# Scattering part of the edges, moving record groups between stages, and turning edge attributes in pairs in a graph network kernel

## The reference, cut to what matters

```python
edge_index = jnp.stack([src, dst])
x = x + _L0_gnn_ref(_layernorm(x), edge_index, ...)   # two gin convolutions
x = x + _L0_ffn_ref(...)                              # slice attention
x = x + _L1_gnn_ref(...)                              # graph attention
x = x + _L1_ffn_ref(...)                              # 8 experts, 2 per node
x = x + _L2_gnn_ref(..., edge_attr_64, ...)           # edge update, below
x = x + _L2_ffn_ref(...)                              # 32 experts, 1 per node
x = x + _L3_gnn_ref(..., src, dst, edge_type_8)       # relations
x = x + _L3_ffn_ref(...)

def _gin_conv(x, src, dst, n, W1, b1, gamma, beta, W2, b2):
    agg = jax.ops.segment_sum(x[src], dst, num_segments=n)
    h = jax.nn.relu(_batchnorm((x + agg) @ W1 + b1, gamma, beta))
    return jax.nn.relu(h @ W2 + b2)

# in _L2_gnn_ref, with row, col = edge_index
edge_in = jnp.concatenate([h[row], h[col], edge_attr], axis=-1)
msg = jax.nn.relu(edge_in @ W1.T + b1) @ W2.T + b2
agg = jax.ops.segment_sum(msg, row, num_segments=h.shape[0])
```

## Time and profile before

| | |
|---|---|
| median of 3 runs | 5867.91 us (5867.34 to 5868.26) |
| the profiled execution | 5852.53 us |
| its span, from the first to the last instruction | 5850.8 us |
| busy: PE, DVE, ACT, POOL | 4793.1, 3170.6, 1333.6, 3178.7 us |
| mean granted clock of TensorE | 0.879 of 2.4 GHz |
| stage of placing | about 93 to 331 us of the span |
| edge update, the loop over quads | about 3672 to 4330 us of the span |

### The profile page before, as it was taken

One profiled execution on the slowest core, in us unless ns is written; L12 is line 12 of the kernel. 1 busy time (PEld: TensorE's weight loads), 2 busy tenths in 40 slices (PEclk: granted clock), 3 DMA queues, 4 the chain that ended last, 5 costly groups with the idle time before them and its releaser, 6 DMA issues. The chain is left out here.

```text
span 5850.8 us, 74399 instructions
## 1 busy us (share of the span) xinstructions
PE 4793.1 (82%) x20458; PEld 2904.0 (50%) x20459; DVE 3170.6 (54%) x7606; ACT 1333.6 (23%) x3259; POOL 3178.7 (54%) x3560
## 2 busy tenths in 40 slices
PE   7968887788768599979985998999997678888674
PEld 2223434433345411118864997788874433333364
DVE  8964444444355577768984114566667433444432
ACT  4940002000032222222213333333332121000121
POOL 3237774777615577746633776667630212777324
PEclk7979999999978755559997999999998789999887
DMA  5013332333411267765525765333330533333265
GB/s 214 11 56 105 103 104 66 106 105 105 95 29 37 78 204 216 216 198 149 159 79 187 219 219 153 112 115 114 114 73 1 154 118 125 105 105 104 50 195 170
DMA packets 392381, 711.85 MB, mean 122 GB/s; under 512 B 117999, under 2 KB 257327, under 8 KB 391663
## 3 DMA queue, kind: packets, MB, share of 16 engines
q0 software_dynamic: 131680, 340.14, 21.3%
q1 hardware_dynamic: 257152, 364.49, 19.5%
q10 hardware_dynamic: 3216, 3.28, 0.2%
HBM read 532.97 MB, written 174.69 MB: 121 GB/s over the span
## 5 line engine op out<-in xcount | busy, mean ns | idle before, releaser
L795 PE MATMUL ps<-wide 128*128 128x256 f32 x2640 | 915.2, 429 | 309.8 <-DMA wide<-table,src 179.8
L822 DVE TENSOR_TENSOR wide<-wide,ps 128x256 f32 x1320 | 555.0, 420 | 968.2 <-PE ps L795 965.2
L780 POOL DMA_INDIRECT wide<-table,src x880 | 846.0, 961 | 276.5 <-PE ps L795 205.0
L795 PEld LDWEIGHTS ps<-wide 128*128 128x128 f32 x2640 | 405.4, 189 | 834.4 <-DMA wide<-table,src 547.4
L792 PE MATMUL ps<-zerow,zerob 128*128 128x440 bf16 x2640 | 712.1, 352 | 27.8 <-DVE wide L127 27.8
L780 POOL DMA_INDIRECT wide<-table_rel,rel x440 | 423.4, 962 | 332.4 <-ACTq L96 198.7
L2777 POOL DMA_INDIRECT work<-table,work x440 | 448.3, 1019 | 190.9 <-issue 106.7
L1669 POOL DMA_INDIRECT wide<-table_gat,src x440 | 427.0, 970 | 135.3 <-issue 133.9
L792 PEld LDWEIGHTS ps<-zerow,zerob 128*128 128x128 bf16 x2640 | 259.2, 98 | 221.9 <-DVE wide L127 29.5
L1838 POOL TENSOR_TENSOR wide<-wide,work 128x1024 f32<-128x1024 f32 x110 | 222.2, 2020 | 197.3 <-ACT work L1822 197.3
L1763 DVE TENSOR_REDUCE work<-ps 128x8 f32<-128x1024 f32 x220 | 269.0, 1223 | 103.9 <-PE ps L1729 100.2
(11 more groups left out here) (522 smaller groups left out, 8647.0 us busy)
## 6 DMA issues: line engine op xcount, KB each, us to landing
edge_rows<-wide SPq DMA_DIRECT2D x110, 532.0 KB, 3.2
wide<-edge_rows SPq DMA_DIRECT2D x110, 532.0 KB
normed<-in_L_ffn_W SPq DMA_DIRECT2D x42, 1024.0 KB
table_rel<-wide SPq DMA_DIRECT2D x25, 1024.0 KB, 4.4
wide<-in_L_ffn_expert_w SPq DMA_DIRECT2D x90, 256.0 KB, 3.1
work<-rec SPq DMA_DIRECT2D x110, 136.0 KB, 2.1
rec<-work SPq DMA_DIRECT2D x27, 544.0 KB, 16.3
normed_T<-in_L_ffn_W SPq DMA_DIRECT2D x14, 1024.0 KB
```

The source lines that it names most:

```text
L780: nc.gpsimd.indirect_dma_start(rows[:, w % RT, :], None, table, bass.IndirectOffsetOnAxis(ap=index[:, w:w + 1], axis=0)).then_inc(gathered ...
L795: nc.tensor.matmul(m.PS[:, w % (2 * Q), 0:D], S[:, w % RT, :], rows[:, w % RT, :], start=True, stop=True).then_inc(summed, 1)
L822: v.tensor_tensor(at, at, m.PS[:, s, 0:D], ALU.add).then_inc(added, 1)
```

## The change

Three things are changed.

First, in `place_edges`, the first 112 of the 416 edge tiles (`STRAIGHT`) no longer go through one-hot products. POOL scatters their two numbers (8 bytes a row) to a table in DRAM, `placed`, that was filled with zeros in an earlier stage; SP loads the table back (`back`), and DVE adds it to what the products of the other 304 tiles gave. For that DVE makes the index `where`, and `pairs`, ahead of its loop, and has two more additions behind it. POOL does its scatters ahead of the record groups.

Second, only groups 0 to 2 are sent in `place_edges`. Groups 3 and 4 go to `linear_features` of the first convolution, 5 and 6 to that of the second, 7 and 8 to `gin_output` of the second. Their loads stand on SP behind the stage's own weights. Groups from 9 stay where they were.

Third, in `edge_update`, SP loads attributes and ends with two DMAs into two buffers, so that the attributes of two edge tiles lie side by side: 128 columns. PE turns such a pair with one transpose instead of two. `wa` becomes 128x512 with the 64x256 weights twice on its diagonal, and one product of 512 columns serves two edge tiles. POOL fills it with zeros, and SP waits for that before it loads the weights and then the records.

```diff
-PLACED = 9
+PLACED = 3
+IN_GIN = 2
+STRAIGHT = 112
+BEGUN = PLACED + 3 * IN_GIN
@@ place_edges
-            for t in range(ET):
+            for t in range(STRAIGHT, ET):
...
         def _(pool):
+            pool.wait_ge(m.placed_blanked, 16)
+            pool.wait_ge(paired, 3)
+            for t in range(STRAIGHT):
+                nc.gpsimd.indirect_dma_start(m.placed, bass.IndirectOffsetOnAxis(ap=where_i[:, t:t + 1], axis=0),
+                                             pairs[:, t, :], None).then_inc(scattered, 16)
             pool.wait_ge(m.rec_blanked, 16 * -(-WP // (BLANK // 4)))
...
+            sp.wait_ge(scattered, 16 * STRAIGHT)
+            sp.dma_start(back, m.placed.rearrange("(p w) c -> p w c", p=P)).then_inc(returned, 16)
...
+            c.step(v.scalar_tensor_tensor(where, m.row_e[:, first], float(WP), m.col_e[:, first], ALU.mult, ALU.add))
+            v.tensor_copy(where_i, where).then_inc(paired, 1)
+            v.tensor_copy(pairs[:, :, 0], both[:, first]).then_inc(paired, 1)
+            v.tensor_copy(pairs[:, :, 1], near[:, first]).then_inc(paired, 1)
...
-            c2.step(v.tensor_tensor(code, below[0][:, 1:WP], below[0][:, 0:WT], ALU.subtract))
-            c2.step(v.scalar_tensor_tensor(source, below[1][:, 1:WP], float(HALF), below[1][:, 0:WT], ALU.add,
-                                           ALU.subtract))
+            dve.wait_ge(returned, 16)
+            c2.step(v.tensor_tensor(upper[0], below[0][:, 1:WP], back[:, 0:WT, 0], ALU.add))
+            c2.step(v.scalar_tensor_tensor(upper[1], below[1][:, 1:WP], float(HALF), back[:, 0:WT, 1], ALU.add, ALU.add))
+            c2.step(v.tensor_tensor(code, upper[0], below[0][:, 0:WT], ALU.subtract))
+            c2.step(v.tensor_tensor(source, upper[1], below[1][:, 0:WT], ALU.subtract))
@@ the groups in the convolutions
+class RecordsBeside:
...
+    def loads(self, sp):
+        for u, g in enumerate(self.groups):
+            load_group(sp, self.attr, self.records, g, u, self.arrived)
+
+    def sends(self, pool):
+        send_groups(self.nc, pool, self.m, self.records, self.groups, self.arrived, self.sent, self.filled)
+        for u in range(IN_GIN):
+            pool.wait_ge(self.sent[u], 16 * SG)
@@ edge_update
-            sp.dma_start(wa[0:EA, :], w1[2 * D:2 * D + EA, :]).then_inc(loaded, 16)
+            sp.wait_ge(blanked, 1)
+            for side in range(2):
+                sp.dma_start(wa[side * EA:(side + 1) * EA, side * D:(side + 1) * D], w1[2 * D:2 * D + EA, :]
+                             ).then_inc(loaded, 16)
...
-                sp.dma_start(rec[:, u * Q:(u + 1) * Q, :], r[:, bass.ds(j * Q, Q), :]).then_inc(came[u], 16)
+                sp.dma_start(ends[:, u * Q:(u + 1) * Q, :], r[:, bass.ds(j * Q, Q), EA:EA + 2]).then_inc(came[u], 16)
+                sp.dma_start(attrs[:, u * Q * EA:(u + 1) * Q * EA].rearrange("p (s c) -> p s c", s=Q),
+                             r[:, bass.ds(j * Q, Q), 0:EA]).then_inc(came[u], 16)
...
-                    mm = te.transpose(m.PS[0:EA, 1, s * P:(s + 1) * P], rec[:, u * Q + s, 0:EA], m.ident[:])
+                for k in range(PAIRS):
+                    at = (u * PAIRS + k) * P
+                    mm = te.transpose(m.PS[:, 1, k * P:(k + 1) * P], attrs[:, at:at + P], m.ident[:])
...
-                    te.matmul(at, ST[:, k, :], tile_at(by_src, tiles[s]), start=True, stop=False)
-                    mm = te.matmul(at, attT[:, k, :], wa, start=False, stop=True)
+                for k in range(PAIRS):
+                    te.matmul(m.PS[:, 2 + k, :], attT[:, u % RS * PAIRS + k, :], wa, start=True, stop=False)
+                    for s in range(2 * k, 2 * k + 2):
+                        at = m.PS[:, 2 + k, s % 2 * D:(s % 2 + 1) * D]
+                        mm = te.matmul(at, ST[:, u % RS * Q + s, :], tile_at(by_src, tiles[s]), start=False,
+                                       stop=(s % 2 == 1))
```

More of the change, by code:

```diff
@@ L458, in place_edges @@
         below = [view(m.BB, o + 5 * WT + ET + k * WP, WP) for k in range(2)]
+        o += 5 * WT + ET + 2 * WP
+        upper = [view(m.BB, o + k * WT, WT) for k in range(2)]
+        back = view(m.BB, o + 2 * WT, WP, 2)
+        pairs = view(m.BB, o + 2 * WT + 2 * WP, STRAIGHT, 2)
+        where = view(m.BB, o + 2 * WT + 2 * WP + 2 * STRAIGHT, STRAIGHT)
+        where_i = view(m.BB, o + 2 * WT + 2 * WP + 3 * STRAIGHT, STRAIGHT).bitcast(I32)
+        first = slice(0, STRAIGHT)
         block = st.block()
@@ L521, in _ @@
                           skip_group_check=True)
-            for t in range(ET):
-                pe.wait_ge(hot, t + 1)
-                pe.wait_ge(stepped, t + 1)
+            for t in range(STRAIGHT, ET):
+                pe.wait_ge(hot, t - STRAIGHT + 1)
+                pe.wait_ge(stepped, t - STRAIGHT + 1)
                 for k in range(2):
@@ L562, in send_groups, with __init__, prepare @@
             after(n)
+class RecordsBeside:
+    def __init__(self, nc, m, attr, first, at):
+        self.nc, self.m, self.attr = nc, m, attr
+        self.groups = range(first, first + IN_GIN)
+        self.records = view(m.WS, at, IN_GIN * SG, EA + 4)
+    def prepare(self, st):
+        self.arrived, self.sent, self.filled = st.sems("arrived", IN_GIN), st.sems("sent", IN_GIN), st.sem("filled")
+    def loads(self, sp):
[5 more added lines that the diff above has]
+            pool.wait_ge(self.sent[u], 16 * SG)
 def blank_records(nc, pool, m, buf, blanked, stored):
@@ L966, in _, with linear_features @@
                 nc.vector.tensor_copy(dst[:, t, :], m.PS[:, t % U, 0:D]).then_inc(taken, 1)
-def linear_features(nc, m, srcT, weight, bias, dstT, gamma, beta):
+def linear_features(nc, m, srcT, weight, bias, dstT, gamma, beta, beside):
     BANKS = 8
@@ L990, in _ @@
             sp.dma_start(gb[:, 1, :], beta).then_inc(loaded, 16)
+            beside.loads(sp)
+        @block.gpsimd
+        def _(pool):
+            beside.sends(pool)
         @block.tensor
@@ L1034, in _, with gin_output @@
             c.step(v.tensor_tensor(m.coef[:, :, 1], gb[:, 1, :], std, ALU.subtract))
-def gin_output(nc, m, zT, weight, bias, into_residual, table):
+def gin_output(nc, m, zT, weight, bias, into_residual, table, beside=None):
     with Stage(nc) as st:
@@ L1045, in gin_output @@
         total = view(m.WS, U * D + (KD + 1) * D, U, D)
+        if beside is not None:
+            beside.prepare(st)
         block = st.block()
@@ L1113, in gin @@
         linear_features(nc, m, m.XT, a[f"L0_gnn_W{conv}a"], a[f"L0_gnn_b{conv}a"], zT, a[f"L0_gnn_g{conv}"],
-                        a[f"L0_gnn_bt{conv}"])
-        gin_output(nc, m, zT, a[f"L0_gnn_W{conv}b"], a[f"L0_gnn_b{conv}b"], last, None if last else m.table)
+                        a[f"L0_gnn_bt{conv}"],
+                        RecordsBeside(nc, m, a["edge_attr_64"], PLACED + int(last) * IN_GIN, 1280))
+        gin_output(nc, m, zT, a[f"L0_gnn_W{conv}b"], a[f"L0_gnn_b{conv}b"], last, None if last else m.table,
+                   RecordsBeside(nc, m, a["edge_attr_64"], PLACED + 2 * IN_GIN, 3584) if last else None)
 def slice_attention(nc, m, a):
@@ L1224, in _ @@
             sp.wait_ge(loaded, 48)
-            for n in range(BESIDE - PLACED):
+            for n in range(BESIDE - BEGUN):
                 if n >= 2:
                     sp.wait_ge(sent[n % 2], n // 2 * 16 * SG)
-                load_group(sp, a["edge_attr_64"], records, PLACED + n, n % 2, arrived)
+                load_group(sp, a["edge_attr_64"], records, BEGUN + n, n % 2, arrived)
             for u in range(2):
-                sp.wait_ge(sent[u], len(range(u, BESIDE - PLACED, 2)) * 16 * SG)
+                sp.wait_ge(sent[u], len(range(u, BESIDE - BEGUN, 2)) * 16 * SG)
         @block.gpsimd
@@ L1236, in _ @@
             ins.then_inc(oned, 1)
-            send_groups(nc, pool, m, records, range(PLACED, BESIDE), arrived, sent, filled)
+            send_groups(nc, pool, m, records, range(BEGUN, BESIDE), arrived, sent, filled)
         @block.scalar
```

54 lines of the change are left out of this document (28 added, 26 removed).

## The result

The changed kernel took 5806.98 us (median of 4 runs, 5800.60 to 5810.32) against 5868.09 us (4 runs, 5867.34 to 5874.42): a ratio of 0.9892, 95% interval 0.9881 to 0.9904, 61 us less. The prediction was 5795 us, with a range of 5778 to 5816. The experiments then ran on chips 4, 7, 2 and 11, where the kernel before takes 6561 to 6626 us. The changed kernel was 0.9% slower than it on chip 4, and close variants of it were 0.7 to 0.9% slower on the others. The chip of the result is not on record. I call it chip 0, and whether it is another chip or one of the four in another condition is not known. The first part of what follows is chip 0's, the rest is mostly on why the sign turns.

What follows compares the result with a forecast made beforehand. ACT was taken to bound the placing at 0.553 us a tile, PE's column stream the edge update. -59.3 (placing) + 0.5 (convolutions) - 13.7 (edge update) = -72.5 us, so 5867.9 becomes 5795.4 us; range 5778 to 5816.

Steps and rivals of the forecast that it cites:

- The direction and the sum: Whole kernel: faster, by 72.5 us in sum; chance of faster 0.95, of slower 0.04.
- the loop: Edge update: paired transposes save 0.155 us a round over 108 rounds, -16.7 us.
- The placing: Placing: 112 tiles fewer on ACT, DVE and PE; next stage starts at 272.5 instead of 331.74 us, -59.3 us.
- the moved groups: Both `linear_features` and second `gin_output`: record scatters hidden behind the stages' own work, +0.5 us, with 0 to +4.
- The range's lower end: Whole kernel: 5778 us, from the bounds of -62 in the placing and -24 in the edge update with the likely start.
- Products and DVE's tail: Placing's end: products run until 263, DVE's closing work begins at 263.0 and ends at 270.1 us.
- POOL's groups: Placing's end: three record groups, last start at 269.2, landing at 271.4 us, closing the stage 1.3 us behind DVE.
- the lower bound of 0.435: Edge update, transposes of a round: all weight loads hidden, 0.435 us instead of 0.66, -24.3 us.
- The rival in which loads pace the transposes: Edge update: weight loads set the bf16 transposes' pace, turning 0.655 us, edge update +3, kernel 5812 us; chance 0.16.
- Its start: Edge update's start: larger fill and two DMAs a quad make the first records later, +3 us (1.5 to 5).
- The rival that ends slower: Placing: small scatters queue; above a step of 1.92 us the kernel is slower, 5899 if each must land; chance 0.04.
- the silent one: Placing: unstated assumption that POOL's scatters cost the products nothing, so 112 tiles save the full 61.9 us.

Runs made afterwards that it cites:

- the run without groups: Changed kernel with no record group in the placing and 122 scattered edge tiles instead of 112, chip 7: 6680.01 us, ratio 1.0092 to the kernel before.
- fewer updates: Kernel before with PE telling ACT and DVE only after every fourth edge tile of the placing that buffers are free, chip 2: 6566.48 us, ratio 0.9996.
- groups stay: Changed kernel with all nine record groups in the placing, none in the convolutions, chip 4: 6669.53 us, ratio 1.0168 to the kernel before.
- after: The changed kernel itself, here run unchanged again on chip 4: 6616.27 us, ratio 1.0091 to the kernel before.

## Why the prediction was right, and where it was not

**The direction and the sum** were right on chip 0: 61 us by the medians where 72.5 were forecast, inside the range. Part of that is luck. By the table of stages, the stretch ahead of the loop cost 7.9 us more than forecast and the loop gave 7.6 more, which nearly cancel. The placing gave 3.8 less, the moved groups cost 1.5 more, and 19 us went in stages that nobody had changed. By the two traces alone the change is worth 48 us, which would be 5820 us and outside the range; the 13 us by which the two traced executions stand differently to their medians bring it in. The range's lower end is a slip too: the bounds it names give 5867.9 - 62 - 24.3 + 3 = 5785, not 5778.

**The placing.** Products and DVE's tail came within 0.3 us: the tail ran from 262.74 to 270.2, forecast 263.0 to 270.1. POOL's step was (236.94 - 96.40) / 111 = 1.266 us, forecast 1.268, so the 8-byte scatters cost what those of 272 bytes do. POOL's groups were the mis-sized term. The second record scatter waited 2.19 us where 0.30 is usual. Last start 271.95 instead of 269.2, and 4.05 us from there to the next stage instead of 3.25: together the 3.5 us by which the stage started late (276.0 against 272.5). POOL closes the stage some 4.7 us behind DVE (276.00 less 270.2 and the 1.05 of before), not 1.3. That POOL is what ends the stage on chip 0 is read from this trace alone, since on the four chips the products end it.

SP had issued the load of the placed table at 239.05, just ahead of that wait, which looks like its cause. Other traces speak against it. With all groups in the placing, SP issues that load at 304.19 and the wait of 2.19 us stands at the same scatter:

```profile
238.14 0.98 POOL L586 DMA_INDIRECT rec<-work,record  x1 [0.51 <-issue]
241.32 0.97 POOL L586 DMA_INDIRECT rec<-work,record  x1 [2.19 <-issue]
```

With 56 scatters the load goes out at 169.07, 0.12 us ahead of the first record scatter, and no wait follows:

```profile
169.19 0.98 POOL L586 DMA_INDIRECT rec<-work,record  x1 [0.52 <-issue]
170.48 0.96 POOL L586 DMA_INDIRECT rec<-work,record  x1 [0.30 <-issue]
```

What the traces share is the count: the wait stands at the 114th indirect DMA that POOL issues in the program, in the run without groups too (2.98 us, between two scatters of line 489). The kernel before issues 72 in its placing, the run with 56 scatters 80, and neither has such a wait. Why it comes at that count is open.

**The moved groups** were costed at +0.5 and came to +2.0. The two `linear_features` make 1.1 us of it: together they take 59.7 to 60.3 us in the traces without groups in them, 61.3 here and up to 64.8 on the four chips, measured by VectorE. In `gin_output` 2 POOL is last: that stage takes 28.5 to 29.2 us from its first instruction in all traces without groups in it, 30.9 here and 37 to 41 on the four chips. Timeline of POOL there, and of DVE at its end:

```profile
1607.29 0.98 POOL L586 DMA_INDIRECT rec<-work,record  x1 [5.59 <-DMA work<-in_edge_attr]
...
1627.42 0.96 POOL L586 DMA_INDIRECT rec<-work,record  x1 [0.30 <-issue]
```

```profile
1629.31 0.42 DVE L1158 SCALAR_TENSOR_TENSOR residual<-work,residual 128x256 f32<-128x256 f32 x1
1631.95 1.73 DVE L685 BATCH_NORM_STATS2 work<-residual 128x6 f32<-128x256 f32 x5 [2.22 <-PEq L101]
```

DVE waits 2.22 us for the next stage. The first scatter starts 6.2 us after the stage does (1601.05), where 4.9 were forecast: the attributes came later than the 4.06 us from the earlier trace rows allowed.

**The edge update.** The loop gained 24.3 us, not 16.7: all weight loads hide. The turning takes 0.44 us, which is the lower bound of 0.435 and not my 0.505. The 0.06 for a 16-bit load was too much, and the first f32 load stands in the open for nothing. The rival in which loads pace the transposes is out, since its turning would be 0.655. The Trainium skill's rule for loads ("TensorE: Matmul & The Clock Gate", section LDWEIGHTS) does not hold against this trace, as a pace: four 16-bit transposes with their loads stand 0.055 us apart. Each of these loads is 0.10 us long in the trace, but the next one starts before it ends.

**Its start** was forecast at +3 and came to +3.5 (from the stage's first instruction to its first inner product 8.56 us before, 12.07 after). But the front grew by 7.4 us more. Timeline of POOL and DVE there:

```profile
3597.14 5.62 POOL L2634 MEMSET wide<- 128x6600 f32 x1
3597.23 5.56 DVE L2657 TENSOR_SCALAR work<-work 128x5 f32<-128x5 f32 x1
3602.83 0.21 ACT L2706 ACTIVATE work<-work 128x5 f32<-128x5 f32 x1 [6.90 <-DVE work L2657]
```

A vector operation of 0.17 us is held for as long as the fill runs, and ACT behind it. In the trace of before the fill, 5.62 us too, met other operations. No run of the fill in pieces on chip 0 backs this. The Trainium skill ("SBUF — State Buffer", section SBUF: two separate sides) says of the pair of ports that VectorE and GpSimd share that it is an exclusive lock, held for a whole instruction, when VectorE runs in a mode with two ports; these rows agree, with an operation that I take to be in it.

**The rest** of the 48 us is 19 us lost in stages whose code is the same: 6.2 in the second gates, 9.2 in the three aggregates, 2.3 in the first gates, others of both signs. The second gates took 21.6 us with the pairs alone on chip 4, and 26.6 us with the kernel before and fewer updates on chip 2, so they have two lengths and the change need not be what picks one. The rest stays open; part of it is the 13 us by which the two profiled executions stand differently to their medians.

**The rival that ends slower** was put at 0.04, with scatters that queue and a step above 1.92 us. On the four chips the kernel and its close variants are slower by 0.7 to 0.9%, but not for that: POOL's step stays at 1.265. The step of the prediction that fails there is the silent one, that a scatter on POOL costs the products nothing. A scattered tile saves the products 0.553 us, and its 1.27 us of POOL hold them for nine tenths of it (1 - 0.553 / 5.60), an estimated 1.14 us. Three runs agree in size: 48 record scatters fewer, with their groups, are 65 us of POOL and gave 58.4 us (groups stay against after, 0.90); 56 edge scatters fewer gave 39.4 us plus the 31 us of added products, over 71 us of POOL (0.99); 33 us of groups out and 12.7 us of scatters in gave 23.0 less 5.5 over 20.3 us (0.86). By these figures the change pays only where the products are held for less than 0.553 / 1.27 = 0.44 of POOL's time.

**The pairs on those chips.** One round of the changed kernel on chip 4, PE:

```profile
4506.00 0.38 PE L2859 MATMUL ps<-identb,work 128*128 128x128 bf16 x4
4506.22 0.39 PE L2863 MATMUL ps<-ident,work 128*128 128x128 f32 x2
4506.44 0.59 PE L2872 MATMUL ps<-wide 128*128 128x512 f32 x1
```

The turning is 0.44 us as on chip 0, yet on chip 4 the loop takes 692 to 700 us with the pairs and 693 without, and on chip 2 it takes 702 with them and 690 without. Windows of the loop on chip 4, without the pairs and then with them:

```profile
4300.00:4900.00 600.00, 572.73 (x3060) 493.45 (x3061) 387.67 (x673) 204.79 (x384) 386.63 (x383) 0.99 0.37 107
```

```profile
4300.00:4900.00 600.00, 561.50 (x2483) 405.86 (x2482) 384.38 (x666) 182.88 (x380) 379.91 (x380) 0.97 0.43 105
```

PE is busy for less and POOL makes as many gathers, 383 and 380. So what PE saves goes into waits there; for what, is not shown.

**What stays open** is what POOL's DMAs use up on the four chips and did not on chip 0. The DMA engines are nearly idle (share 0.02 in the window). The trace has a hint: in the same 100 us of the placing it holds 1807 records of semaphore updates on chip 0, 1264 of them for the scatters, 16 each, and 143 on chip 4; over the whole execution 80,877 and 38,725. The program makes as many on both. All seven traces of the four chips with 112 scatters or more hold 141 to 146 in that window, whatever the ring and the number of PE's updates: one record in 0.70 us, eight for a tile of 5.60 us. With POOL silent there are 542, three for each of 181 tiles. So either the updates or the recording of them is congested, and each run on record lists a span and a granted clock, so each was a recorded execution. The Trainium skill ("NOTIFIC — the notification-queue block", section Overflow: three behaviours, one of which stalls the engine) says that the block's internal pipeline holds its producers back rather than lose a record. That fits the standing engines; the missing records speak against it. Whether the products stand in an execution without recording was not tried, and with it stays open how much of the sign is the chip's own.

## What to carry to other kernels

Work put on an idle engine is free only if nothing couples it to the engine that it relieves, so weigh it against the stage in both directions: what it saves there (0.553 us a tile), and what it would cost if that engine stood for as long as the added work runs (1.27 us). Where an engine waits longer than its peer's rows explain, change the ring's depth and the number of updates one at a time, and then silence the suspect: the last was the run that showed that the scatters are at fault, though not what they use up. When a wait seems to follow from an event beside it, look for a trace in which the event lies elsewhere. Time a change on more than one chip before calling it a gain.

## What the hardware showed that was not expected

- While POOL issued indirect DMAs, ACT, DVE and PE were held to one tile in 5.60 us on chips 4, 7, 2 and 11, instead of one in 0.553 us on chip 0, with POOL's own step the same (1.265 us). With POOL silent the placing took 238.5 us on chip 11, as in the kernel before on chip 0, where POOL issues. Beside 243 us of POOL's own arithmetic and copies the third stage of the graph attention took 410 to 413 us everywhere.
- In a placing with 122 or more indirect DMAs from POOL the 114th waited 2.19 to 2.98 us instead of 0.30 us, whatever stood around it; in one with 72 or 80 no such wait came.
- Scatters of 8 bytes a row run at 1.266 us a step, those of 272 at 1.268.
- Four 16-bit transposes with their weight loads start 0.055 us apart; the loads hide.
- A 128x5 vector operation took 5.56 us under a POOL fill of 5.62 us, 0.17 us without (seen once).
